# Channel attention: weighing in column quarters, and dividing after 32 by 32 transposes

## The chip, the cores and the metric

One core of a Trainium2 chip runs the whole program. The metric is the device time of one execution in microseconds, median of several. TensorE's clock is granted by the chip at one of two levels, 2.4 or 1.2 GHz; the profile shows the share granted (1.00 or 0.50).

## The reference, cut to what matters

Two layers of gated cross attention and feed-forward on x, 16 batch elements of 64 tokens by 256 features: gated attention, a mixture of experts, channel attention, a 4-bit MLP. The change is in the third, where the 64 tokens play the part of channels: 8 heads of 8 channels, and 256 features attend to 256 features.

```python
# q = layernorm(x), k = v = ctx_2048; per batch element 64 x 256
qh = q.reshape(B, 8, 8, 256)
kh = k.reshape(B, 8, 8, 256)
vh = v.reshape(B, 8, 8, 256)
qk = einsum('bhdq,bhdl->bhql', qh, kh) / sqrt(8)
ret = einsum('bhql,bhdl->bhdq', softmax(qk, axis=-1), vh)
x = x + tanh(g_xattn[1]) * gamma * ret.reshape(B, 64, 256)
```

## The kernel before, in words

Four stages follow one another; each is a block in which the five engines run their own instruction queues and wait for each other through semaphores. A tile of x holds two batch elements, i counts tiles, par is the half. The order of work in channel attention is written out by hand for each engine.

Per batch element, heads go in four pairs. For the next one it computes `row_scores` (L1504, matmuls at L1516: 32 rows of the array per head, since q and k are each split in a high and a low part and four products of 8 channels are laid side by side). VectorE reduces them to a maximum per query (`maxima`, L1676, L1684); the bank is reused, so the next pair's row scores wait for that. After four pairs `turn_maxima` (L1520, L1526) transposes the maxima and VectorE copies them to mT (`take_maxima`, L1689). For the present batch element TensorE computes `column_scores` (L1529): minus the maxima (L1539) plus the scores with keys on the partitions (L1544). ScalarE takes the exponent of each head's 512 columns (L1624). TensorE also replicates the rows of q and k for later pairs (`replicate`, L1492, L1499), which ScalarE copies (L1614).

`weigh` (L1549, L1559) multiplies values and exponents, contraction over 128 keys. Its stationary operand is a slice of vmask, 128 keys by 64 columns: the first 32 columns hold a head's 8 channels of values in the place of that head among four (zeros elsewhere), the other 32 hold ones in the same place. So PSUM rows 0 to 31 collect weighed values of four heads, rows 32 to 63 the sums of the exponents, once per channel; heads 4 to 7 do the same in rows 64 to 127. Both halves of the array's columns work on one pair of heads; four pairs accumulate. The matmuls are float32, and the profile shows two records for each: 8 for a pair, 32 for a batch element. The exponents have four buffers. vmask has a buffer per par, whose value columns GpSimd fills (`values`, L1650, L1659).

VectorE then inverts the sums (`invert`, L1691, two reciprocals of 128 columns over all 128 partitions, L1695), scales (`take_values`, L1697, two operations of 32 partitions, L1703) and adds to x (`add_values`, L1707, L1710). These stand between the maxima of the next batch element. At the end of the stage VectorE, ScalarE and GpSimd already begin the next stage's weights and its first statistics (`vector_stats_ahead`, L1106), which wait on `weighed`.

The order on TensorE for a batch element:

```python
for pair in range(C_HEADS // 2):
    row_scores(ni, npar, pair)
    column_scores(i, par, pair, first)
    if pair == 0: replicate(ni, npar, 1)
    if pair == 2: replicate(i + 1, par, 0)
    if pair >= 1: weigh(i, par, pair - 1, first)
turn_maxima(ni, npar)
weigh(i, par, C_HEADS // 2 - 1, first)
```

Of the kernel before, what the change touches and what calls it, by code (L numbers as in the profile page):

```python
# [15 lines left out]
ALU = mybir.AluOpType  # L16
# [9 lines left out]
P = 128  # L26
# [867 lines left out]
class Context:  # L894
# [3 lines left out]
    def __init__(self, nc, k, a, st):  # L898
        sb = lambda n, shape, dt: st.enter_context(nc.sbuf_tensor("context_" + n, shape, dt))
        self.nc, self.k, self.a = nc, k, a  # L900
        self.rows = sb("rows", [P, TILES, HID], F32)
        self.hi = sb("hi", [P, TILES, HID], F32R)
        self.lo = sb("lo", [P, TILES, HID], F32R)
        self.spread_in = sb("spread_in", [P, 16, P], F32)
        self.minus_in = sb("minus_in", [P, 2, P], F32)
        self.spread = sb("spread", [P, 16, P], F32R)
        self.minus = sb("minus", [P, 2, P], F32R)
        self.mx = sb("mx", [P, CH, P], F32)
        self.vmask = sb("vmask", [P, 2, CH, C_HEADS, 2 * C_ROWS], F32)
        self.rows_in, self.spread_arrived, self.minus_arrived, self.high, self.zeroed = [  # L910
            st.enter_context(nc.semaphore("context_" + n)) for n in ("rows_in", "spread_arrived", "minus_arrived", "high", "zeroed")]

# [20 lines left out]
    def gpsimd(self, pool):  # L933
        nc = self.nc
        nc.gpsimd.memset(self.vmask[:], 0.0).then_inc(self.zeroed, 1)
        nc.gpsimd.memset(self.mx[:], 0.0)
        pool.wait_ge(self.zeroed, 1)
        for par in range(2):
            for head in range(C_HEADS):
                col = C_ROWS + head % C_GROUP * C_DIM  # L940
                nc.gpsimd.memset(self.vmask[:, par, :, head, col:col + C_DIM], 1.0)


class Router:
# [100 lines left out]
class FourBitWeights:  # L1045
# [59 lines left out]

    def vector_stats_ahead(self, dve, x_done):  # L1106

        dve.wait_ge(x_done, 8)
        self.turn.vector_stats(dve, halves=(0,))

    def vector_ahead(self, dve):
# [330 lines left out]
def channel_attention(nc, k, a):  # L1442
# [8 lines left out]
    with ExitStack() as st:  # L1451
# [12 lines left out]

        qk_rows = sb("qk_rows", [P, 2, 2, 2, HID], F32R)
        mT = sb("mT", [P, HID], F32R)
        probs = sb("probs", [P, 4, 512], F32)
        inv = sb("inv", [P, HID], F32)
        part = sb("part", [P, HID], F32)
        s = {n: sem(n) for n in ("stats_done", "rstd_step", "row_normed", "c_turned", "c_copied", "h_high", "rest_high", "h_low", "gain_ready",  # L1470
                                 "rep_ready", "rep_copied", "a_ready", "a_reduced", "mt_ready", "mt_copied", "b_ready",
                                 "exp_done", "pv_done", "values_set", "inverted", "weighed", "out_taken")}
        A_BANK, B_BANK, REP_BANK, MT_BANK = 0, 2, 5, 6
        OUT_BANK = (4, 7)
        block = st.enter_context(nc.Block())
# [13 lines left out]
        def _(pe):  # L1489
# [56 lines left out]
                        if c == CH - 1:  # L1546
                            last.then_inc(s["b_ready"], 1)

            def weigh(i, par, pair, first=False):  # L1549

                pe.wait_ge(s["exp_done"], C_HEADS * (2 * i + par) + 2 * pair + 2)
                if pair == 0:
                    pe.wait_ge(s["values_set"], 2 * i + par + 1)
                    if not first:

                        pe.wait_ge(s["out_taken"], 2 * i + par - 1)
                for c in range(CH):
                    for e in range(2):
                        last = mm(ps[64 * e:64 * e + 64, OUT_BANK[par], 0:HID], vmask[:, par, c, pair + 4 * e, :],  # L1559
                                  probs[:, (2 * pair + e) % 4, c * HID:c * HID + HID],  # L1560
                                  start=(pair == 0 and c == 0), stop=(pair == C_HEADS // 2 - 1 and c == CH - 1))
                        if c == CH - 1:
                            last.then_inc(s["pv_done"], 1)

            def batch(i, par, first=False, scores_after=True, rows_after=True):
                ni, npar = (i, 1) if par == 0 else (i + 1, 0)
                for pair in range(C_HEADS // 2):
                    if scores_after:
                        row_scores(ni, npar, pair)
                    column_scores(i, par, pair, first)  # L1570
                    if pair == 0 and scores_after:

                        replicate(ni, npar, 1)
                    if pair == 2 and rows_after:
                        if first:

                            pe.wait_ge(s["h_low"], 2)

                        replicate(i + 1, par, 0)
                    if pair >= 1:  # L1580
                        weigh(i, par, pair - 1, first)
                if scores_after:
                    turn_maxima(ni, npar)
                weigh(i, par, C_HEADS // 2 - 1, first)

            for j in range(2 * CH):
                half, c = divmod(j, CH)
# [18 lines left out]
                batch(i, 1)  # L1606
            batch(LAST, 0, rows_after=False)
            batch(LAST, 1, scores_after=False, rows_after=False)

        @block.scalar  # L1610
        def _(act):
# [4 lines left out]
            def batch(i, par, first=False, scores_after=True, rows_after=True):  # L1616
                ni, npar = (i, 1) if par == 0 else (i + 1, 0)
                for head in range(C_HEADS):
                    n = C_HEADS * (2 * i + par) + head
                    act.wait_ge(s["b_ready"], n + 1)  # L1620
                    if not (first and head < 4):

                        act.wait_ge(s["pv_done"], n - 3)
                    nc.scalar.activation(probs[:, head % 4, :], ps[:, B_BANK + head % 2, :], ACT.Exp,  # L1624
                                         scale=float(C_DIM) ** -0.5).then_inc(s["exp_done"], 1)
# [23 lines left out]
        def _(pool):  # L1649
            def values(i, par, first=False):  # L1650
                if not first:

                    pool.wait_ge(s["pv_done"], C_HEADS * (2 * i + par - 1))

                flat = vmask[:, par].rearrange("p c h m -> p c (h m)")
                for head in range(C_HEADS):
                    col = head * 2 * C_ROWS + head % C_GROUP * C_DIM
                    src = cT[:].rearrange("p c (n b m) -> p c n b m", b=2, m=64)[:, :, i, par, head * C_DIM:head * C_DIM + C_DIM]
                    last = nc.gpsimd.tensor_copy(flat[:, :, col:col + C_DIM], src)  # L1659
                last.then_inc(s["values_set"], 1)  # L1660
# [14 lines left out]
        def _(dve):  # L1675
# [15 lines left out]
            def invert(i, par, part_of):  # L1691
                b = 2 * i + par
                dve.wait_ge(s["pv_done"], C_HEADS * (b + 1))
                cols = slice(part_of * P, part_of * P + P)
                nc.vector.reciprocal(inv[:, cols], ps[:, OUT_BANK[par], cols]).then_inc(s["inverted"], 1)  # L1695

            def take_values(i, par):  # L1697
                b = 2 * i + par
                dve.wait_ge(s["inverted"], CH * (b + 1))
                for half in range(2):  # L1700
                    rows, sums = [slice(at, at + C_ROWS) for at in (64 * half, 64 * half + C_ROWS)]
                    to = slice(64 * par + C_ROWS * half, 64 * par + C_ROWS * half + C_ROWS)
                    last = nc.vector.scalar_tensor_tensor(part[to, :], ps[rows, OUT_BANK[par], 0:HID], gain[rows, 0:1], inv[sums, :],  # L1703
                                                          ALU.mult, ALU.mult)
                last.then_inc(s["out_taken"], 1)

            def add_values(i, par):  # L1707
                mine = slice(64 * par, 64 * par + 64)
                dve.wait_ge(s["out_taken"], 2 * i + par + 1)
                nc.vector.tensor_tensor(x[mine, i, :], x[mine, i, :], part[mine, :], ALU.add).then_inc(s["weighed"], 1)  # L1710

            def finish(i, par):
                invert(i, par, 0)
                invert(i, par, 1)
                take_values(i, par)
                add_values(i, par)

            def batch(i, par, first=False, scores_after=True):
                ni, npar = (i, 1) if par == 0 else (i + 1, 0)
# [5 lines left out]
                if first:  # L1725
# [1 line left out]
                    dve.wait_ge(s["rest_high"], 1)  # L1727
                    nc.vector.tensor_tensor(h_lo[:, 1:TILES], h[:, 1:TILES], h_hi[:, 1:TILES].bitcast(F32), ALU.subtract
                                            ).then_inc(s["h_low"], 1)
                else:  # L1730
                    invert(*done, 0)
                maxima(ni, npar, 1)
                if not first:
                    invert(*done, 1)
                maxima(ni, npar, 2)
                if not first:
                    take_values(*done)
                maxima(ni, npar, 3)
                take_maxima(ni, npar)
                if not first:  # L1740
                    add_values(*done)

            row_stats(nc, dve, x, stats, mv, s["stats_done"], 0)
            nc.vector.tensor_scalar(gain[:], vec[:, S_GAMMA:S_GAMMA + 1], k.gain[:, 1:2], None, ALU.mult).then_inc(s["gain_ready"], 1)
# [14 lines left out]
            batch(LAST, 1, scores_after=False)  # L1759
            k.ffn.vector_ahead(dve)  # L1760
            finish(LAST, 1)


def build(nc, a, out, stages):
# [88 lines left out]
```

## Time and profile before

| | us |
|---|---|
| median of 3 runs | 1088.43 (1088.19 to 1090.18) |
| the profiled execution | 1089.46 |
| its span | 1087.70 |
| TensorE matmul busy | 981.8 (90%) |
| VectorE busy | 749.8 (69%) |
| ScalarE busy | 539.2 (50%) |
| GpSimd busy | 268.0 (25%) |
| mean granted clock | 0.947 |

PE is TensorE's matmuls, PEld its weight loads, DVE VectorE, ACT ScalarE, POOL GpSimd. Busy matmuls overlap, and their ends are modelled. A group "x8" in a timeline is eight records merged; "128*64" is rows by columns of the array that are in use. In square brackets stands how long the engine had been idle, and what ended it.

### The profile page before, as it was taken

What the parts mean: (1) busy time and instruction counts of PE and PEld (TensorE: products, weight loads), DVE (VectorE), ACT (ScalarE), POOL (GpSimd) and SP (SyncE); (2) the same over time, 40 slices, a digit from 0 to 9 for tenths busy, and PEclk for the clock granted to TensorE, in tenths of its full rate; (3) what the DMA queues carried; (4) which work ended last, traced back from release to release, by engine and by line L of the source; (5) the groups of instructions that cost most, each with busy time, mean ns of one, the idle gap of its engine ahead of it and who ended that gap; (6) DMA issues with size and microseconds to landing.
All of it is one profiled execution on the core that took longest, in us unless ns stands there. A gap on an engine that the chain in (4) does not pass through costs nothing. (4 is left out here: it accounts for less than half of the span.)

```text
span 1087.7 us, 19039 instructions
## 1 busy us (share of the span) xinstructions
PE 981.8 (90%) x6752; PEld 822.5 (76%) x6752; DVE 749.8 (69%) x1301; ACT 539.2 (50%) x1655; POOL 268.0 (25%) x416
## 2 busy tenths in 40 slices
PE   3689999999999999956899999995999999699998
PEld 3579999999999998855677777773666665577776
DVE  8858878777878787776544454445688888666653
ACT  5566666666666665622433333323455554233332
POOL 2133333333333333302422222202010111323130
PEclk8799999999999999976799999997899998799999
DMA  5001020101010100004111111001000000110001
GB/s 180 1 2 59 2 59 2 59 2 59 2 60 1 60 4 18 2 1 176 44 47 47 47 46 46 3 0 59 1 1 0 0 0 2 58 59 30 29 0 39
DMA packets 22823, 35.40 MB, mean 33 GB/s; under 512 B 2016, under 2 KB 19552, under 8 KB 21600
## 3 DMA queue, kind: packets, MB, share of 16 engines
q1 hardware_dynamic: 22464, 34.38, 9.6%
q8 instruction: 41, 0.67, 0.3%
q14 instruction: 30, 0.25, 0.1%
q10 hardware_dynamic: 288, 0.10, 0.0%
HBM read 33.42 MB, written 1.05 MB: 32 GB/s over the span
## 5 line engine op out<-in xcount | busy, mean ns | idle before, releaser
L251 PE MATMUL ps<-wt_hi,xq 128*128 128x256 f32 (+1 forms) x512 | 124.7, 278 | 13.0 <-issue 10.3
L251 PE MATMUL ps<-wt_lo,xq 128*128 128x256 f32 (+1 forms) x512 | 122.2, 281 | 0.0
L458 ACT ACTIVATE square<-ps 128x128 bf16<-128x128 f32 x384 | 100.6, 293 | 39.7 <-PE ps L251 39.6
L251 PEld LDWEIGHTS ps<-wt_hi,xq 128*128 128x128 f32 x512 | 98.4, 192 | 17.2 <-issue 15.3
L1624 ACT ACTIVATE ca_probs<-ps 128x512 f32<-128x512 f32 x128 | 69.5, 595 | 82.8 <-PE ps L1544 82.8
L251 PEld LDWEIGHTS ps<-wt_lo,xq 128*128 128x128 f32 x512 | 98.9, 193 | 0.0
L1684 DVE TENSOR_REDUCE context_mx<-ps 128x4 f32<-128x1024 f32 x64 | 76.9, 1201 | 26.4 <-PE ps L1516 26.4
L596 POOL TENSOR_TENSOR rstd<-rstd,half_neg 128x6 f32<-128x6 f32 x64 | 87.2, 1362 | 5.0
L1210 POOL TENSOR_TENSOR moe_w_lo<-moe_w_all,moe_w_hi 128x384 fp32r<-128x384 f32 x48 | 54.8, 1176 | 135.4 <-ACT moe_w_hi L1311 135.4
L458 ACT ACTIVATION_READ_ACCUMULATOR square<-ps 128x1 f32 x384 | 86.0, 225 | 0.0
L1375 DVE TENSOR_TENSOR moe_act_g<-moe_act_g,ps 128x512 f32<-128x512 f32 x48 | 33.0, 687 | 70.5 <-PE ps L1246 70.5
L669 DVE TENSOR_TENSOR qn<-ps,rstd 128x512 f32<-128x512 f32 x64 | 44.2, 690 | 49.4 <-POOL rstd L596 49.4
L1246 PE MATMUL ps<-moe_hT_hi,moe_w_hi 128*128 128x512 f32 x192 | 76.7, 399 | 0.6 <-POOL moe_w_lo L1210 0.6
L1327 ACT CAST moe_in_hi<-moe_inner 128x512 fp32r<-128x512 f32 x48 | 29.8, 621 | 94.6 <-DVE moe_inner L1378 82.7
L1246 PE MATMUL ps<-moe_hT_hi,moe_w_lo 128*128 128x512 f32 x192 | 75.8, 395 | 0.0
L1246 PE MATMUL ps<-moe_hT_lo,moe_w_hi 128*128 128x512 f32 x192 | 75.7, 394 | 0.0
L1559 PE MATMUL ps<-ca_probs,context_vmask 128*64 128x256 f32 x512 | 74.2, 415 | 0.0
L315 PE MATMUL ps<-wp_hi,catq 128*128 128x256 f32 x256 | 66.5, 298 | 7.2 <-DVE catq L93 7.2
L276 PE MATMUL ps<-kT,qT 128*128 128x64 f32 x512 | 64.2, 281 | 3.4 <-ACT kT L474 1.9
L276 PEld LDWEIGHTS ps<-kT,qT 128*128 128x128 f32 x512 | 62.3, 199 | 3.8 <-issue 2.1
L315 PE MATMUL ps<-wp_lo,catq 128*128 128x256 f32 x256 | 64.8, 292 | 0.0
L592 POOL TENSOR_TENSOR rstd<-sumsq,eps 128x6 f32<-128x6 f32 x64 | 15.1, 236 | 197.1 <-ACT square L458 197.1
(225 smaller groups left out, 2685.8 us busy)
## 6 DMA issues: line engine op xcount, KB each, us to landing
moe_w_all<-in_experts SPq DMA_DIRECT2D x8, 1152.0 KB, 5.4
wp_rows<-in_wproj SPq DMA_DIRECT2D x16, 256.0 KB, 2.9
ffn_codes<-in_codes SPq DMA_DIRECT2D x8, 384.0 KB, 3.2
ffn_w_scales<-in_code_scales SPq DMA_DIRECT2D x8, 384.0 KB, 3.9
w_rows<-in_wq SPq DMA_DIRECT2D x8, 256.0 KB, 3.7
w_rows<-in_wqx SPq DMA_DIRECT2D x8, 256.0 KB, 3.9
w_rows<-in_w_kv_x SPq DMA_DIRECT2D x16, 128.0 KB, 3.6
x_rows<-in_x SPq DMA_DIRECT2D x2, 512.0 KB, 5.1
```

Source lines behind the costliest of these rows:

```text
L251: last = mm(ps[:, first + bank, col:col + n], left[:, c, tokens], w[:, c, wcol:wcol + n], start=(j == 0), stop=(j == len(steps) - 1))
L276: last = mm(ps[:, S_BANK, b * SEQ:b * SEQ + SEQ], qT[:, r, batch].rearrange("p h s -> p (h s)"), kT[:, r, batch * SEQ:batch * SEQ + SEQ], ...
L315: last = mm(ps[:, CAT_BANK + j, q * HID:q * HID + HID], catq[:, f // HPG, f % HPG, t * P:t * P + P], w[:, f, :], start=(n == 0), stop=(n = ...
L458: last = nc.scalar.activation(square[:, j, :], ps[:, bank, (j % 4) * P:(j % 4) * P + P], ACT.Square, scale=float(HD) ** -0.5, accum_out=su ...
L596: nc.gpsimd.tensor_tensor(rstd[:, i % 2, :], rstd[:, i % 2, :], k.half_neg[:, 0:6], ALU.pow).then_inc(s["rstd_ready"], 1)
L669: nc.vector.tensor_tensor(qn[:, i % 2, 0:4, :], ps[:, bank, :].rearrange("p (h d) -> p h d", h=4), rstd[:, i % 2, 0:4].unsqueeze(2).broadc ...
L1210: last = nc.gpsimd.tensor_tensor(w_lo[:, b, cols], w_all[:, b, cols], w_hi[:, b, cols].bitcast(F32), ALU.subtract)
L1246: last = mm(ps[:, bank, :], w[:, b, col:col + P], h[:, c, tokens], start=(n == 0), stop=(n == len(steps) - 1))
L1375: nc.vector.tensor_tensor(act_g[:, half, :], act_g[:, half, :], ps[:, U_BANK, :], ALU.mult).then_inc(s["gated"], 1)
L1559: last = mm(ps[64 * e:64 * e + 64, OUT_BANK[par], 0:HID], vmask[:, par, c, pair + 4 * e, :], probs[:, (2 * pair + e) % 4, c * HID:c * HID ...
L1624: nc.scalar.activation(probs[:, head % 4, :], ps[:, B_BANK + head % 2, :], ACT.Exp, scale=float(C_DIM) ** -0.5).then_inc(s["exp_done"], 1)
L1684: nc.vector.tensor_reduce(dst, ps[:, A_BANK:A_BANK + 2, :].rearrange("p e (q l) -> p e q l", q=CH), AX.X, ALU.max).then_inc(s["a_reduced"], 1)
```

## The change

TensorE weighs four heads at a time, each in 32 of the array's 128 columns. The stationary operand is 128 keys by 32 columns: 16 columns hold the 8 channels of a head in one of two places, and one of the columns 16 and 17 holds ones, so a head's sum of exponents now takes one row of PSUM instead of eight. Quarter 2t + e holds heads 2 turn + t + 4 e for turn 0 and 1. There are two blocks of `weigh` per batch element instead of four: turn 0 at the end of its own batch, turn 1 in pair 1 of the next one. The exponents get a buffer for each of the 8 heads, and ScalarE waits for whole blocks.

Since sums and values now lie in different rows of one quarter, VectorE transposes the PSUM tile in blocks of 32 by 32 (`turn_values`), so that both lie in the columns of one partition; takes the reciprocals of 16 numbers per partition (`invert`); scales values by gain and reciprocal, writing them in the order of channels (`scale_values`, two operations of 64 partitions); and, once for two batch elements, transposes back (`turn_back`) and adds 128 rows to x. The count that `vector_stats_ahead` waits for follows, since `weighed` now rises once per tile. The diff, cut to its core:

```diff
-        self.vmask = sb("vmask", [P, 2, CH, C_HEADS, 2 * C_ROWS], F32)
+        self.vmask = sb("vmask", [P, 2, CH, C_HEADS, C_ROWS], F32)
...
-                col = C_ROWS + head % C_GROUP * C_DIM
-                nc.gpsimd.memset(self.vmask[:, par, :, head, col:col + C_DIM], 1.0)
+                col = 2 * C_DIM + head // 2 % 2
+                nc.gpsimd.memset(self.vmask[:, par, :, head, col:col + 1], 1.0)
...
-        probs = sb("probs", [P, 4, 512], F32)
-        inv = sb("inv", [P, HID], F32)
+        probs = sb("probs", [P, C_HEADS, 512], F32)
+        turned = sb("turned", [P, HID], F32)
+        inv = sb("inv", [P, HID // 32, 2], F32)
+        weighed = sb("weighed", [P, HID], F32)
...
+            def weigh(i, par, turn, first=False):
+
+                pe.wait_ge(s["exp_done"], C_HEADS * (2 * i + par) + 4 * turn + 4)
+                if turn == 0:
                     pe.wait_ge(s["values_set"], 2 * i + par + 1)
                     if not first:
 
                         pe.wait_ge(s["out_taken"], 2 * i + par - 1)
                 for c in range(CH):
+                    for quarter in range(4):
+                        t, e = divmod(quarter, 2)
+                        last = mm(ps[32 * quarter:32 * quarter + 32, OUT_BANK[par], 0:HID], vmask[:, par, c, 2 * turn + t + 4 * e, :],
+                                  probs[:, 4 * turn + quarter, c * HID:c * HID + HID],
+                                  start=(turn == 0 and c == 0), stop=(turn == 1 and c == CH - 1))
+                last.then_inc(s["pv_done"], 1)
...
+                done = (i - 1, 1) if par == 0 else (i, 0)
...
+                    if pair == 1 and not (first and par == 0):
+                        weigh(*done, 1)
...
-                    if pair >= 1:
-                        weigh(i, par, pair - 1, first)
+                weigh(i, par, 0, first)
                 if scores_after:
                     turn_maxima(ni, npar)
-                weigh(i, par, C_HEADS // 2 - 1, first)
...
+            weigh(LAST, 1, 1)
...
+                    if not first and head % 4 == 0:
+
+                        act.wait_ge(s["pv_done"], 2 * (2 * i + par) + head // 4 - 1)
+                    nc.scalar.activation(probs[:, head, :], ps[:, B_BANK + head % 2, :], ACT.Exp,
...
-                    pool.wait_ge(s["pv_done"], C_HEADS * (2 * i + par - 1))
+                    pool.wait_ge(s["pv_done"], 2 * (2 * i + par - 1))
...
+            def turn_values(i, par):
                 b = 2 * i + par
+                dve.wait_ge(s["pv_done"], 2 * (b + 1))
+                nc.vector.transpose(turned[:], ps[:, OUT_BANK[par], 0:HID]).then_inc(s["out_taken"], 1)
+
+            def invert(i, par):
+                dve.wait_ge(s["out_taken"], 2 * i + par + 1)
+                nc.vector.reciprocal(inv[:], turned[:].rearrange("p (b r) -> p b r", r=32)[:, :, 2 * C_DIM:2 * C_DIM + 2]
+                                     ).then_inc(s["inverted"], 1)
+
+            def scale_values(i, par):
+                dve.wait_ge(s["inverted"], 2 * i + par + 1)
+                to = slice(64 * par, 64 * par + 64)
+                for t in range(2):
+                    rows = slice(64 * t, 64 * t + 64)
+                    dst = weighed[to, :].rearrange("p (b r t d) -> p t b r d", r=2, t=2, d=C_DIM)[:, t]
+                    src = turned[rows, :].rearrange("p (b h r d) -> p h b r d", h=2, r=2, d=C_DIM)[:, 0]
+                    last = nc.vector.scalar_tensor_tensor(dst, src, gain[rows, 0:1],
+                                                          inv[rows].unsqueeze(3).broadcast_to([64, HID // 32, 2, C_DIM]),
                                                           ALU.mult, ALU.mult)
+                last.then_inc(s["scaled"], 1)
+
+            def turn_back(i):
+                dve.wait_ge(s["scaled"], 2 * i + 2)
+                nc.vector.transpose(part[:], weighed[:]).then_inc(s["turned_back"], 1)
+
+            def add_values(i):
+                dve.wait_ge(s["turned_back"], i + 1)
+                nc.vector.tensor_tensor(x[:, i, :], x[:, i, :], part[:], ALU.add).then_inc(s["weighed"], 1)
...
-                else:
-                    invert(*done, 0)
                 maxima(ni, npar, 1)
-                if not first:
-                    invert(*done, 1)
                 maxima(ni, npar, 2)
                 if not first:
-                    take_values(*done)
+                    turn_values(*done)
+                    invert(*done)
                 maxima(ni, npar, 3)
+                if not first:
+                    scale_values(*done)
                 take_maxima(ni, npar)
-                if not first:
-                    add_values(*done)
+                if not first and par == 0:
+                    turn_back(i - 1)
+                    add_values(i - 1)
```

## Rows read from the trace of the kernel before

**Rows 1.** The page: busy time, share of the span and instructions of each engine.
```profile
PE 981.8 (90%) x6752; PEld 822.5 (76%) x6752; DVE 749.8 (69%) x1301; ACT 539.2 (50%) x1655; POOL 268.0 (25%) x416
```

**Rows 2.** Timeline of a steady batch: start, length, engine, line, what; idle before.
```profile
834.22 0.51 PE L1516 MATMUL ps<-ca_qk_rows 32*128 32x256 f32 x4
...
834.77 1.23 DVE L1684 TENSOR_REDUCE context_mx<-ps 128x4 f32<-128x1024 f32 x1 [0.58 <-PE ps L1516]
...
835.30 1.09 ACT L1624 ACTIVATE ca_probs<-ps 128x512 f32<-128x512 f32 x2 [2.30 <-PE ps L1544]
...
836.05 0.50 PE L1516 MATMUL ps<-ca_qk_rows 32*128 32x256 f32 x4 [0.20 <-DVE context_mx L1684]
...
837.11 1.08 PE L1559 MATMUL ps<-ca_probs,context_vmask 128*64 128x256 f32 x8
...
838.13 0.50 PE L1516 MATMUL ps<-ca_qk_rows 32*128 32x256 f32 x4
...
844.06 0.51 PE L1516 MATMUL ps<-ca_qk_rows 32*128 32x256 f32 x4
```

**Rows 3.** Windows: length, busy time of PE, PEld, DVE, ACT, POOL, then granted clock.
```profile
760.00:765.00 5.00, 4.70 (x24) 3.65 (x26) 3.90 (x5) 1.67 (x3) 0.00 (x0) 0.50 0.00 0
765.00:770.00 5.00, 5.00 (x28) 3.12 (x24) 2.29 (x2) 2.11 (x4) 0.00 (x0) 0.50 0.00 0
772.00:775.00 3.00, 3.00 (x29) 1.84 (x28) 1.65 (x2) 1.09 (x2) 0.00 (x0) 1.00 0.00 0
910.00:912.00 2.00, 1.78 (x16) 0.92 (x14) 1.44 (x3) 0.95 (x2) 0.00 (x0) 1.00 0.00 0
912.00:914.00 2.00, 1.17 (x12) 0.54 (x8) 1.97 (x9) 0.79 (x2) 0.00 (x0) 1.00 0.00 0
914.00:916.00 2.00, 1.65 (x12) 1.15 (x14) 1.97 (x5) 1.18 (x3) 1.20 (x2) 0.83 0.00 0
916.00:918.00 2.00, 2.00 (x12) 0.99 (x10) 1.95 (x4) 0.26 (x2) 0.00 (x0) 0.50 0.04 8
918.00:920.00 2.00, 2.00 (x10) 0.86 (x12) 1.90 (x5) 1.02 (x2) 0.00 (x0) 0.50 0.00 0
```

**Rows 4.** Timeline at the granted clock 0.50, the stage's first scores and weighing.
```profile
760.30 0.69 PE L1526 MATMUL ps<-ident,context_mx 128*128 128x128 f32 x2 [1.33 <-DVE context_mx L1684]
...
760.92 0.80 PE L1516 MATMUL ps<-ca_qk_rows 32*128 32x256 f32 x4
...
765.39 1.98 PE L1559 MATMUL ps<-ca_probs,context_vmask 128*64 128x256 f32 x8
...
767.29 0.80 PE L1516 MATMUL ps<-ca_qk_rows 32*128 32x256 f32 x4
...
768.88 0.58 PE L1499 MATMUL ps<-ca_h_hi,context_spread 128*128 128x256 f32 x1
...
770.03 1.98 PE L1559 MATMUL ps<-ca_probs,context_vmask 128*64 128x256 f32 x8
```

**Rows 5.** Timeline of the stage's last batch.
```profile
916.69 0.79 PE L1539 MATMUL ps<-ca_mT,context_minus 32*128 32x512 f32 x2
...
917.84 1.98 PE L1559 MATMUL ps<-ca_probs,context_vmask 128*64 128x256 f32 x8
917.94 1.09 ACT L1624 ACTIVATE ca_probs<-ps 128x512 f32<-128x512 f32 x2 [1.74 <-PE ps L1544]
...
927.46 0.42 DVE L1710 TENSOR_TENSOR x_rows<-x_rows,ca_part 64x256 f32<-64x256 f32 x1
```

**Rows 6.** VectorE operations by tile: duration ns min/median/max, first and last start, forms.
```profile
L1695 DVE RECIPROCAL ca_inv<-ps x32: 894/944/958, 776.9 to 925.5; 128x128 f32<-128x128 f32 x32
L1703 DVE SCALAR_TENSOR_TENSOR ca_part<-ps,ca_gain,ca_inv x32: 471/478/483, 780.9 to 926.9; 32x256 f32<-32x256 f32 x32
...
L1689 DVE CAST ca_mT<-ps x16: 424/426/427, 761.0 to 911.5; 128x256 fp32r<-128x256 f32 x16
...
L1021 DVE RECIPROCAL route_col<-route_col x1: 203/203/203, 521.0 to 521.0; 128x8 f32<-128x8 f32 x1
```

More of the change, by code:

```diff
@@ L1106, in vector_stats_ahead @@
     def vector_stats_ahead(self, dve, x_done):
-        dve.wait_ge(x_done, 8)
+        dve.wait_ge(x_done, TILES // 2)
         self.turn.vector_stats(dve, halves=(0,))
@@ L1471, in channel_attention @@
                                  "rep_ready", "rep_copied", "a_ready", "a_reduced", "mt_ready", "mt_copied", "b_ready",
-                                 "exp_done", "pv_done", "values_set", "inverted", "weighed", "out_taken")}
+                                 "exp_done", "pv_done", "values_set", "inverted", "scaled", "turned_back", "weighed", "out_taken")}
         A_BANK, B_BANK, REP_BANK, MT_BANK = 0, 2, 5, 6
@@ L1547, in column_scores @@
                             last.then_inc(s["b_ready"], 1)
-            def weigh(i, par, pair, first=False):
-                pe.wait_ge(s["exp_done"], C_HEADS * (2 * i + par) + 2 * pair + 2)
-                if pair == 0:
+            def weigh(i, par, turn, first=False):
+                pe.wait_ge(s["exp_done"], C_HEADS * (2 * i + par) + 4 * turn + 4)
+                if turn == 0:
                     pe.wait_ge(s["values_set"], 2 * i + par + 1)
@@ L1557, in weigh @@
                 for c in range(CH):
[L1558 to L1563, printed above, removed]
+                    for quarter in range(4):
[4 more added lines that the diff above has]
+                last.then_inc(s["pv_done"], 1)
             def batch(i, par, first=False, scores_after=True, rows_after=True):
                 ni, npar = (i, 1) if par == 0 else (i + 1, 0)
+                done = (i - 1, 1) if par == 0 else (i, 0)
                 for pair in range(C_HEADS // 2):
@@ L1620, in batch @@
                     act.wait_ge(s["b_ready"], n + 1)
-                    if not (first and head < 4):
-                        act.wait_ge(s["pv_done"], n - 3)
-                    nc.scalar.activation(probs[:, head % 4, :], ps[:, B_BANK + head % 2, :], ACT.Exp,
+                    if not first and head % 4 == 0:
+                        act.wait_ge(s["pv_done"], 2 * (2 * i + par) + head // 4 - 1)
+                    nc.scalar.activation(probs[:, head, :], ps[:, B_BANK + head % 2, :], ACT.Exp,
                                          scale=float(C_DIM) ** -0.5).then_inc(s["exp_done"], 1)
@@ L1651, in values @@
                 if not first:
-                    pool.wait_ge(s["pv_done"], C_HEADS * (2 * i + par - 1))
+                    pool.wait_ge(s["pv_done"], 2 * (2 * i + par - 1))
                 flat = vmask[:, par].rearrange("p c h m -> p c (h m)")
                 for head in range(C_HEADS):
-                    col = head * 2 * C_ROWS + head % C_GROUP * C_DIM
+                    col = head * C_ROWS + head // 2 % 2 * C_DIM
                     src = cT[:].rearrange("p c (n b m) -> p c n b m", b=2, m=64)[:, :, i, par, head * C_DIM:head * C_DIM + C_DIM]
@@ L1689, in take_maxima @@
                 nc.vector.tensor_copy(mT[:], ps[:, MT_BANK, 0:HID]).then_inc(s["mt_copied"], 1)
-            def invert(i, par, part_of):
+            def turn_values(i, par):
                 b = 2 * i + par
[L1693 to L1703, printed above, removed]
-                                                          ALU.mult, ALU.mult)
-                last.then_inc(s["out_taken"], 1)
@@ L1707, in add_values @@
[L1707 to L1710, printed above, removed]
+                dve.wait_ge(s["pv_done"], 2 * (b + 1))
[4 more added lines that the diff above has]
+                                     ).then_inc(s["inverted"], 1)
@@ L1712, in finish @@
+            def turn_back(i):
[4 more added lines that the diff above has]
+                nc.vector.tensor_tensor(x[:, i, :], x[:, i, :], part[:], ALU.add).then_inc(s["weighed"], 1)
             def finish(i, par):
-                invert(i, par, 0)
-                invert(i, par, 1)
-                take_values(i, par)
@@ L1716, in finish @@
-                add_values(i, par)
+                turn_values(i, par)
+                invert(i, par)
+                scale_values(i, par)
             def batch(i, par, first=False, scores_after=True):
@@ L1761, in _ @@
             finish(LAST, 1)
+            turn_back(LAST)
+            add_values(LAST)
 def build(nc, a, out, stages):
```

## Prediction

> **What bounds the kernel now.** I read the page first: TensorE (PE) is busy 90% of the span, VectorE (DVE) 69% [rows 1]. The change touches one stage, channel attention, from about 745 to 928 us, so I went to the order of time in its steady state. One batch element (a "batch" below) takes from one `row_scores` of pair 0 to the next, 834.22 to 844.06, 9.85 us [rows 2]; there are 16. TensorE sets that pace: in a whole batch it waits only once, 0.20 us before 836.05, for the maxima [rows 2]. A block of `weigh` is one row of 8 matmul records, 837.11 to the next row at 838.13, 1.02 us [rows 2], four times per batch: 4.08 of 9.85 us. Two chains run close behind. The maxima: `row_scores` at 834.22, reduction 834.77 to 836.00, next `row_scores` at 836.05, so 1.83 us per pair at best. The exponents: 1.09 us per pair on ScalarE (ACT) from 835.30 [rows 2].
>
> Then the granted clock. The stage's first scores run at 1.2 GHz and the clock stays there from 760 to 770, though TensorE is busy 4.70 and 5.00 of 5 us; at 772 it is 2.4 GHz [rows 3]. At the end it falls: TensorE was busy 1.78 and 1.17 of 2 us in 910 to 914, in 914 to 916 the grant is mixed, and in 916 to 920 it is 1.2 GHz although TensorE is busy all the time [rows 3]. So in this stage being busy does not by itself bring the clock back, and I look at what TensorE ran in each stretch. From 760.92 to 765.39 it ran score matmuls on 32 of 128 rows and one `replicate`. From 765.39 to 771.93, just before the rise, it ran two weigh blocks of 1.90 and a `replicate` of 1.15: 4.95 of 6.54 us with all 128 rows in use [rows 4]. In the tail, score columns from 916.69 alternate with weigh blocks from 917.84, of 1.90 us again; 1.90 of each 3.05 us is weighing, and the clock stays down [rows 3, 5].
>
> **The change, part by part.** Weighing goes from four blocks of 8 records (64 columns of the array each) to two blocks of 16 records (32 columns each). The count of matmuls and weight loads per batch is the same; the gain exists if four quarters run beside each other as two halves did. *Block of 16:* not in the trace. From below, the block of 8 at the same clock, 1.02 or 1.90 us; from above twice that, 2.04 or 3.80 (quarters no better than halves). I take the lower end: halves and quarters are the same kind of splitting, and each quarter still has four records to run in a row as each half had. By the Trainium skill, page "TensorE: Matmul & The Clock Gate", Part 3, three column tiles gave 2.38 times one; by that efficiency, as an estimate, a block would be 2.4 us at 1.2 GHz and the sum below some 15 us higher.
>
> *Clock.* This decides. What the change removes from TensorE is exactly the work that uses the whole array, while the score matmuls on 32 rows stay. From the rows at 1.2 GHz: row and column scores of a pair 767.29 to 768.88, 1.59; `replicate` 768.88 to 770.03, 1.15; weigh block 765.39 to 767.29, 1.90; turning the maxima 760.30 to 760.92, 0.62 [rows 4]. A changed batch at that clock is 4 x 1.59 + 2 x 1.15 + 2 x 1.90 + 0.62 = 13.08 us. Of it 6.72 us (51%) is work on all 128 rows; the tail, which did not get its clock back, had 62%, and the stretch before the rise 76%. The scores begin at 1.2 GHz in both kernels, and nothing before 765.39 changes. So I forecast that the clock does not come back in this stage, or drops again soon, and that batches take 13.08 instead of 9.85 us.
>
> *VectorE, per batch.* Removed: two reciprocals of 128 columns, 0.94 each [rows 6], two scalings of 0.48 and an addition of 0.42, 3.3 us. Added: a transpose of 256 columns out of PSUM, a reciprocal of 16, two scalings of 128 columns, and every second batch a transpose and an addition of 128x256. The transposes are not in the trace: between 0.20 (the small reciprocal) and 1.9 (two big ones); I take 0.43, the copy of 128x256 from PSUM, the same shape and source. Reciprocal of 16: 0.20, that of 8 columns. Scaling: between 0.20 and 0.48; I take 0.35 [rows 6]. Sum 0.43 + 0.20 + 0.70 + (0.43 + 0.42)/2 = 1.76. With four maxima (4.9) and the copy (0.43) VectorE has 7.1 of 13.08 us to do: hidden at 1.2 GHz, even with each transpose at 1.9. If that cover went (full clock) it would cost up to 0.85 us every second batch, since `turn_back` and `add_values` stand ahead of the next maxima.
>
> *Waits.* `scale_values` is ahead of `take_maxima`, for which `column_scores` of the next batch waits; at 1.2 GHz the weigh block before `turn_maxima` covers it. ScalarE now waits for whole blocks of the batch before (8 buffers), which are long done. GpSimd's copies of the values wait for `pv_done` of the batch before last, and are next needed at the end of a batch: no cost. The memsets of a half-sized `vmask` lie in the expert stage on an engine with 75% idle: no cost. No DMA moves.
>
> **The sum**, against the profiled execution (1089.46 us, span 1087.70; 1.03 above the median of 1088.43).
> - First batch: both kernels start it at 760.92. Changed, it has one weigh block, at its end; the column scores of its third pair wait for the exponents of the second, whose columns end at 765.39: some 0.1 + 1.09 us, to 766.6 [rows 2, 4]. Then 1.0 (columns), 1.15, 1.59, 1.90 and 0.62, with 0.1 between: next batch at 772.95.
> - 13 batches of 13.08 and one of 11.93 (no `replicate` for a later pair): 954.9.
> - Last batch: no row scores; its pairs follow the exponent chain, 916.69 to 917.94 (1.25) and 1.09, 2.4 us each [rows 5]; with the weigh block in pair 1 the last exponent ends at about 965.5, two weigh blocks at 968.2, the VectorE chain (0.43, 0.20, 0.95, 0.43, 0.42 and waits) at 970.8.
> - Before, this was 927.88 [rows 5]. Difference +42.9; 1089.46 + 42.9 = 1132.4; less 1.0 to stand beside the median: **1131**. Own range, with 0.3 us a batch either way: 1124 to 1142.
>
> **Rivals.**
> *B, the clock holds 2.4 GHz (the other side).* For it: the stage before this and the steady state held it with some waits. Then a batch loses 2.04 us of weighing. Pairs 1 to 3, 836.05 to 844.06, go from 8.01 to 5.97, pair 0 stays 1.83: 7.80 [rows 2]. But the waits uncovered: pair 2 without its block is shorter than the maxima's 1.83 (+0.2), pair 0 waits for `take_maxima` and pair 1 for the exponents (+0.35), and every second batch for turn back and addition (+0.3 on average): 8.65. 14 batches from 772.95 end at 893.5, the last takes 13.5, so 907, 21 us less than now: 1067. It decides if TensorE, then with about 1.3 us of waits in 8.65, is enough to hold or regain the clock; against it, 1.17 of 2 us in 912 to 914 was followed by the fall [rows 3]. The Trainium skill, page "TensorE: Matmul & The Clock Gate", Part 1, says that activity releases the throttle and idle time sets it; read as plain busy time that gives this rival. Rows 3 speak against that reading: a TensorE that is busy throughout 916 to 920 stays at 1.2 GHz.
> *C, the clock goes to and fro.* Between B and the forecast in proportion: 1080 to 1120; even with before when a third of the stage is at 1.2 GHz.
> *D, the change doesn't do what it says:* quarters overlap no better than halves. Then a block is 3.80 and 31 blocks add 59 us to the forecast, 1190 (less at full clock, where the time would stay near 1090 with TensorE as busy as now).
>
> **Chances.** Forecast 0.60, B 0.22, C 0.14, D 0.04. The range 1064 to 1144 takes forecast, B and C with their bounds, and leaves out D and thin ends. Faster by over 0.2% (about what a measurement here can tell from no change): B and a third of C, 0.27; within 0.2%: 0.02; slower 0.71.
>
> **What would show it.** Right: granted clock 0.50 from 760 to 930 nearly throughout, `row_scores` of pair 0 every 13 us, TensorE without waits, the weigh block of 16 records 1.9 us long, VectorE idle before the maxima for TensorE, transposes of 0.4 us. Wrong: clock 1.00 over the stage with batches of 8 to 9 us and TensorE waiting for VectorE (B), the clock changing between windows (C), or a block of 16 near 3.8 us (D).

## The result, and the profile after

| | before | changed |
|---|---|---|
| median, us | 1088.31 | 1135.24 |
| range | 1087.04 to 1090.18 | 1131.59 to 1137.78 |
| profiled execution, span | 1089.46, 1087.70 | 1137.69, 1135.9 |
| mean granted clock | 0.947 | 0.868 |

The ratio is 1.0415, 95% interval 1.0392 to 1.0439: 4% slower. The page of the changed kernel, engines and granted clock in 40 slices (its first line answers to [rows 1]):

```profile
PE 1027.8 (90%) x6750; PEld 851.9 (75%) x6752; DVE 731.0 (64%) x1301; ACT 542.6 (48%) x1655; POOL 268.0 (24%) x416
...
PEclk8799999999999999776999999965555555799999
```

TensorE is busy for 46 us more, with the same number of matmuls and half as many blocks of weighing; VectorE for 19 us less. In slices 27 to 33, counted from 0 (767 to 965 us), the granted clock stands at 5 tenths. Windows over the stage, with the columns of [rows 3]:

```profile
760.00:765.00 5.00, 4.81 (x26) 3.75 (x26) 3.90 (x5) 1.67 (x3) 0.00 (x0) 0.50 0.01 3
765.00:770.00 5.00, 4.25 (x26) 3.36 (x26) 2.50 (x3) 2.76 (x5) 0.00 (x0) 0.50 0.00 0
780.00:800.00 20.00, 20.00 (x128) 12.63 (x124) 10.91 (x17) 8.26 (x15) 1.82 (x13) 0.50 0.00 1
...
904.00:908.00 4.00, 3.12 (x24) 1.96 (x22) 2.43 (x4) 1.56 (x3) 0.00 (x0) 0.90 0.00 0
908.00:920.00 12.00, 12.00 (x81) 7.51 (x78) 6.53 (x9) 4.37 (x9) 1.16 (x8) 0.51 0.00 0
```

The clock was down when the scores began, as before, and did not come back at 772. While there were scores to run it rose once, at 904.8, and fell again at 908.2; it rose a second time at 969.6, in the stage's last weighing, 0.2 us before TensorE was through with the stage. A batch in order of time, `row_scores` (now L1518) of pair 0 to that of the next:

```profile
852.08 0.80 PE L1518 MATMUL ps<-ca_qk_rows 32*128 32x256 f32 x4
...
852.19 0.42 DVE L1693 CAST ca_mT<-ps 128x256 fp32r<-128x256 f32 x1 [1.36 <-PE ps L1528]
...
852.75 0.79 PE L1541 MATMUL ps<-ca_mT,context_minus 32*128 32x512 f32 x2
...
855.05 0.80 PE L1518 MATMUL ps<-ca_qk_rows 32*128 32x256 f32 x4
...
856.63 1.94 PE L1562 MATMUL ps<-ca_probs,context_vmask 128*32 128x256 f32 x16
...
858.50 0.80 PE L1518 MATMUL ps<-ca_qk_rows 32*128 32x256 f32 x4
...
861.23 0.80 PE L1518 MATMUL ps<-ca_qk_rows 32*128 32x256 f32 x4
...
862.07 1.23 DVE L1688 TENSOR_REDUCE context_mx<-ps 128x4 f32<-128x1024 f32 x1 [0.87 <-PE ps L1518]
...
862.81 1.94 PE L1562 MATMUL ps<-ca_probs,context_vmask 128*32 128x256 f32 x16
...
864.68 0.69 PE L1528 MATMUL ps<-ident,context_mx 128*128 128x128 f32 x2
...
865.29 0.80 PE L1518 MATMUL ps<-ca_qk_rows 32*128 32x256 f32 x4
```

From 852.08 to 865.29 are 13.21 us, against 9.85 [rows 2] and a forecast of 13.08. Scores and `replicate` of a pair start at 852.08 and give way to the next at 855.05; a block of 16 records takes 1.87 us to the next row (856.63 to 858.50, 862.81 to 864.68), where 8 took 1.90 at this clock [rows 4]. The profile names no wait of TensorE's matmuls for another engine in the batch, and the maxima wait for it (0.87 us before 862.07). One short delay is there all the same: pair 0 takes 2.97 us (852.08 to 855.05), pair 2, with the same work, 2.73 (858.50 to 861.23). In pair 0 the column scores (852.75) begin 0.14 us after VectorE has copied the maxima (852.61); the changed order turns the maxima right before the next batch, with no block of weighing behind it to cover the copy. The profile names this wait where less stands before it: 0.16 us before 905.55, when the clock was up, and 0.52 us before 957.28, in the batch without row scores. VectorE's new work by tile (duration ns min/median/max), first what reads or writes `turned`, then `part`:

```profile
L1712 DVE SCALAR_TENSOR_TENSOR ca_weighed<-ca_turned,ca_gain,ca_inv x32: 332/349/987, 783.9 to 971.1; 64x128 f32<-64x128 f32 x32
L1698 DVE STREAM_TRANSPOSE ca_turned<-ps x16: 437/439/450, 781.2 to 969.9; 128x256 f32<-128x256 f32 x16
L1702 DVE RECIPROCAL ca_inv<-ca_turned x16: 252/252/254, 781.7 to 970.4; 128x16 f32<-128x16 f32 x16
```

```profile
L1719 DVE STREAM_TRANSPOSE ca_part<-ca_weighed x8: 445/445/446, 799.8 to 972.2; 128x256 f32<-128x256 f32 x8
L1723 DVE TENSOR_TENSOR x_rows<-x_rows,ca_part x8: 424/426/624, 800.4 to 972.6; 128x256 f32 x6, 128x256 f32<-128x256 f32 x2
```

And the end of the stage: the fourth row scores of the batch before the last, then score columns, weighing, the transposes and the addition to x:

```profile
952.36 0.80 PE L1518 MATMUL ps<-ca_qk_rows 32*128 32x256 f32 x4 [0.47 <-DVE context_mx L1688]
...
957.28 0.79 PE L1541 MATMUL ps<-ca_mT,context_minus 32*128 32x512 f32 x2 [0.52 <-DVE ca_mT L1693]
...
966.23 3.59 PE L1562 MATMUL ps<-ca_probs,context_vmask 128*32 128x256 f32 x32
...
969.90 0.45 DVE L1698 STREAM_TRANSPOSE ca_turned<-ps 128x256 f32<-128x256 f32 x1 [0.19 <-PE ps L1562]
...
972.17 0.45 DVE L1719 STREAM_TRANSPOSE ca_part<-ca_weighed 128x256 f32<-128x256 f32 x1
972.65 0.62 DVE L1723 TENSOR_TENSOR x_rows<-x_rows,ca_part 128x256 f32<-128x256 f32 x1
```

The last addition ends at about 973.3, before at 927.88 [rows 5]: 45.4 of the 48.2 us of span are lost in this stage. The other 2.8 us lie in the 4-bit MLP, which ran at 1.2 GHz for some 10 us at its start (before: 8) and once more for 3 us at 1000.

### The profile page after: what moved, and what is told of

The parts are those of the page before. It is cut to its first block and busy times, and to the rows that moved or that the text cites. A ratio compares the mean times of both kernels' runs of the same rounds, so it can differ in the third digit from the quotient of the medians.

```text
span 1135.9 us, 18925 instructions
## 1 busy us (share of the span) xinstructions
PE 1027.8 (90%) x6750; PEld 851.9 (75%) x6752; DVE 731.0 (64%) x1301; ACT 542.6 (48%) x1655; POOL 268.0 (24%) x416
## 5 line engine op out<-in xcount | busy, mean ns | idle before, releaser
L601 POOL TENSOR_TENSOR probs<-probs,total 128x512 f32<-128x512 f32 x32 | 33.5, 1047 | 122.7 <-DVE total L703 122.7
```

What stands on the lines that cost most here:

```text
L601: nc.gpsimd.tensor_tensor(probs[:, r], probs[:, r], total[:, r, :].unsqueeze(2).broadcast_to([P, 8, SEQ]), ALU.mult).then_inc(s["probs_rea ...
```

## The experiments

The question was whether the clock is the cause, or only goes along with work that is slow by itself (quarters, transposes, the new order). To move the clock alone, unread matmuls are put where TensorE mostly waits. They write to 256 columns of PSUM banks that nothing reads, so the result is computed as before:

```diff
+            def lead(n):
+                for _ in range(n):
+                    mm(ps[:, OUT_BANK[0], HID:2 * HID], spread[:, 0, :], c_hi[:, 0, :], start=True, stop=True)
+            def fill(i, par, n):
+                for _ in range(n):
+                    mm(ps[:, OUT_BANK[par], HID:2 * HID], spread[0:128, 0, :], h_hi[0:128, i, :], start=True, stop=True)
```

Each is 128 rows by 128 columns by 256; the runs with "32" in their name use `[0:32]` in `fill`.

**A first start, too weak: kick_hold, kick_hold32, kick, kick_before.** `fill(0, 0, 5)` after each `row_scores` of the four before the first batch; the "hold" runs also have `fill(i, par, 4)` after the first `replicate` of a batch and `fill(i, par, 2)` after the second.

> The changed kernel with extra matmuls whose result nobody reads, 128 rows by 128 columns by 256, into free columns of PSUM: 5 after each row_scores of the stage's first batch, where TensorE waits for the maxima anyway, and in every later batch 4 after the first replicate and 2 after the second. Clock theory (the array is used too little for the clock to come back): the granted clock is 1.00 from about 765 us on, a batch takes 8.6 to 9.3 us instead of 13.2, total 1065 to 1080. Rival (quarters, transposes and the new order cost the time themselves, the clock is a bystander): the time does not fall, and the added work makes it 1137 to 1150.

Measured: four executions, three at 1152.1 to 1156.9 with a mean granted clock of 0.862 to 0.867 and one at 1075.2 with 0.948. The start did not lift the clock in most executions. The one at 1075.2, which has no trace, was some 80 us below the others: the first sign that the changed kernel is quick at 2.4 GHz. The profiled one (1152.1) is at 1.2 GHz up to 964 and takes 14.5 us a batch: six unread matmuls of 128 rows in every batch cost 1.3 us there and did not bring the clock back. The median, 1154.4, missed the expectation.

> As kick_hold, in number, place and columns, but each extra matmul has 32 rows instead of 128 (a quarter of the array). Clock theory, with use of the array and not busy time as what counts: the clock stays at 0.50 as in the changed kernel, a batch takes 13.2 plus about 1.3 us, total 1148 to 1162. If it is TensorE's busy time that brings the clock back, this run is as fast as kick_hold.

Measured 1136.1 (1135.8 to 1136.8). The clock stayed low but for two rises of 3.4 us while there were scores to run, and the added matmuls cost less than expected, 1 us over the changed kernel instead of 13 or more: the trace shows the added matmuls running beside the row and column scores (the first of a batch starts at 866.44, the row scores at 866.45), and a batch takes 13.23 us.

> The changed kernel with the extra matmuls of the first batch alone (5 after each row_scores). Clock theory: the clock is 1.00 by about 760 us, drops within one to three batches, and does not come back; total within 15 us below the changed kernel, 1120 to 1137. If only the way in was missing (once at 2.4 GHz the stage holds it), 1060 to 1075.

Measured 1137.8, at the slow edge of what was expected. The clock was not up at the start (it rose for 3.4 us at 827 and at 905), so this tells little.

> The kernel before with the same extra matmuls of the first batch alone. Clock theory: the clock, which came back at 772, is there some 8 to 12 us earlier, and the kernel before holds it: 4 to 7 us faster, 1081 to 1085. Rival: no change, 1088.

Measured 1094.5, ratio 1.0052 (1.0035 to 1.0069): a miss, slower. Its trace has the clock back at 777 instead of 772, so the first batches ran longer at 1.2 GHz. The stage ends 2.2 us later than before (930.0 against 927.9); the rest of the loss lies in the next stage, where the clock falls once more, from 958 to 962. Why the added work did not bring the clock back sooner was not settled, and it speaks against the simple reading that more work on all rows is always enough.

**A strong start: lead_hold, lead_hold32, lead, lead_before.** While TensorE waits for the normed rows its clock is still at 2.4 GHz, and it falls in that gap (changed kernel: no matmul from 744 to 748, clock down at 748). The edit, on top of the above:

```diff
+            lead(40)
             pe.wait_ge(s["h_low"], 1)
             replicate(0, 0, 0, first=True)
...
                 row_scores(0, 0, pair, first=(pair == 0))
-                fill(0, 0, 5)
+                lead(8)
```

> The changed kernel with unread matmuls on the whole array: 40 right after the context is turned, while TensorE waits for the rows and its clock is still at 2.4 GHz, 8 after each row_scores before the first batch, and 4 + 2 in every later batch (as in kick_hold). Clock theory: the clock never falls before the last batch, a batch takes 8.6 to 9.3 us, total 1064 to 1078, in nearly every run. Rival (the new work itself is slow): at least 1130.

Measured: eleven executions, five at 1081.1 to 1089.8 (mean clock 0.933 to 0.947), six at 1148.3 to 1153.5 (0.868 to 0.873). The profiled one is of the second kind, its windows:

```profile
755.00:760.00 5.00, 4.21 (x35) 3.07 (x33) 4.45 (x5) 2.06 (x4) 0.00 (x0) 1.00 0.01 3
760.00:765.00 5.00, 3.90 (x30) 3.22 (x34) 3.14 (x3) 2.28 (x6) 0.00 (x0) 0.75 0.00 0
765.00:770.00 5.00, 5.00 (x32) 3.01 (x25) 1.92 (x3) 1.86 (x4) 0.00 (x0) 0.50 0.01 2
```

The clock was up to 760 and fell while TensorE was busy 3.90 of 5 us: in the first batch pair 1 has no weigh block and TensorE waits for VectorE, 1.63 us before 761.10. What was lost there did not come back in the stage, although the same 4 + 2 matmuls ran in every batch and TensorE was busy all the time (60 of 60 us from 800 to 860, batches of 14.5 us). The five shorter executions have no trace; that they kept the clock through this gap is an inference from their mean clock, and none reached the 1064 to 1078 that was expected.

> As lead_hold, but the 4 + 2 of every later batch have 32 rows. Clock theory, use of the array: the stage begins at 2.4 GHz, loses it within a few batches and stays at 0.50, 1125 to 1145. If busy time holds the clock, 1064 to 1078 as lead_hold.

Measured: five executions, three at 1114.5 to 1116.4 (clock 0.899 to 0.901), two at 1132.8 and 1133.2 (0.878 and 0.877). By the mean clock none kept it. The first three are faster than the expected 1125 to 1145; the profiled one (1133.2) lost the clock at 760 and, while it had scores to run, had it back twice for 3.4 us.

> The changed kernel with the 40 and 4 x 8 at the start alone. Clock theory: begins at 2.4 GHz, falls within one to three batches for want of work in the array and does not come back: 1120 to 1138. If the fall in the gap before the scores was all that was wrong: 1060 to 1075. Its batches at 2.4 GHz, while they last, measure rival B of the prediction, forecast at 8.65 us.

Measured 1132.9 (1131.5 to 1134.2); in its trace the clock, up at the start, falls at 762 and rises again only for 3.4 us at 929.6. Holding it, not only reaching it, is what the changed kernel lacks. The clock fell before a steady batch, so this run does not price one at 2.4 GHz.

> The kernel before with the 40 and 4 x 8 at the start alone. The first two batches run at 2.4 GHz and the kernel holds it as it does now: 4 to 9 us faster, 1079 to 1085. If the clock at the start is worth nothing to it: 1088.

Measured 1087.1, ratio 0.9985 (0.9974 to 0.9996): 2 us, less than expected. The clock fell for 6.8 us at 760 and came back at 767. The stage itself ends 4.6 us earlier than before (923.2 against 927.9), as expected; in the profiled execution 2.7 us of it are lost again in the next stage, whose clock falls once more at 951.

**The clock held throughout: held and held32.** On top of lead_hold, with 6 and 3 in place of 4 and 2:

```diff
                     if pair == 1 and not (first and par == 0):
                         weigh(*done, 1)
+                    if first and par == 0 and pair in (1, 3):
+                        fill(i, par, 12)
+                    if not scores_after:
+                        fill(i, par, 6)
```

> lead_hold lost the clock in the first batch, at pair 1 and 2, where TensorE waits 1.5 us for VectorE. This kernel fills that gap too: 12 unread matmuls on the whole array in pair 1 and in pair 3 of the first batch, 6 + 3 in every batch, 6 per pair in the last one. Clock theory: granted clock 1.00 from the start of the stage to its end in nearly every run, a batch of 8.6 to 9.2 us, total 1062 to 1078, faster than both kernels. Rival (new work is slow): 1130 or more. Rival B of the prediction put a batch at this clock at 8.65 us, with waits of TensorE for VectorE of 0.6 us every second batch.

Measured 1070.9 (1069.2 to 1071.7), ratio 0.9837 (0.9823 to 0.9851), five executions of one kind. Granted clock 1.00 up to 906, the end of the stage:

```profile
780.00:800.00 20.00, 19.57 (x215) 13.53 (x211) 15.38 (x22) 11.68 (x22) 2.94 (x21) 1.00 0.00 1
800.00:860.00 60.00, 58.37 (x605) 41.30 (x605) 47.65 (x70) 35.89 (x68) 7.40 (x52) 1.00 0.00 0
860.00:900.00 40.00, 37.46 (x393) 26.09 (x395) 31.22 (x54) 22.55 (x43) 5.79 (x34) 1.00 0.00 1
```

> The same number and places, but after the start (40 and 4 x 8 on the whole array) the unread matmuls have 32 rows. Clock theory, use of the array: the clock is lost in the first batches and the stage runs at 0.50 nearly throughout, 1125 to 1150. If busy time counts, 1062 to 1078 as held.

Measured 1116.0 (1115.3 to 1116.8), ratio 1.0250, faster than the expected 1125 to 1150. Its windows:

```profile
765.00:770.00 5.00, 5.00 (x39) 3.95 (x42) 1.51 (x2) 2.13 (x5) 0.00 (x0) 0.50 0.00 0
775.00:779.00 4.00, 4.00 (x40) 2.37 (x39) 1.38 (x2) 1.09 (x2) 0.49 (x4) 0.58 0.02 4
...
780.00:800.00 20.00, 19.57 (x215) 13.50 (x215) 16.34 (x26) 12.54 (x24) 2.30 (x16) 1.00 0.00 1
800.00:820.00 20.00, 19.57 (x205) 13.93 (x208) 15.53 (x22) 11.75 (x23) 2.30 (x16) 1.00 0.00 0
820.00:840.00 20.00, 19.72 (x175) 12.90 (x169) 13.56 (x20) 9.55 (x18) 2.29 (x16) 0.74 0.00 0
840.00:860.00 20.00, 20.00 (x135) 13.34 (x135) 9.04 (x14) 8.26 (x15) 1.77 (x13) 0.50 0.00 0
```

From 780 to 800 the two kernels show the same TensorE: 19.57 of 20 us busy, 215 matmuls, clock 1.00. The one with 128 rows keeps the clock to the end of the stage, the one with 32 loses it at 830 and does not get it back while it has scores to run, busy 20 of 20 us. Two things were not expected: it had lost the clock at 765 too and got it back at 778, right behind a block of weighing, with no unread matmul on more than 32 rows; and it then held it for some 50 us. Why it fell at 830 and not before the profile does not show. But number, places and columns are the same; only the rows in use differ, and 45 us hang on it. So busy time alone does not decide it.

What the clock's rises have in common can be read from the traces. In those of the kernel before, the changed kernel and the runs above and below, the clock rises 22 times between the start of the first batch and the end of the stage, each time while matmuls on all 128 rows run or within 0.6 us of their end: a block of weighing, the turning of the maxima that follows one (after: weighing 902.44, turning 904.30, rise 904.8), or twelve unread matmuls (held_before, 763). This fits the forecast's account. It does not say how much of such work is needed: most blocks of weighing are followed by no rise.

**The change at equal clock: held_before.** The kernel before with `lead(40)`, `lead(8)`, `fill(i, par, 12)` in pair 1 of the first batch and 6 in the last, none between.

> The kernel before with the start of held: 40 and 4 x 8 unread matmuls on the whole array, 12 in pair 1 of the first batch, 6 in the last; none in between, since the kernel before holds 2.4 GHz by itself. Gives the kernel before with the clock up from the start: 1078 to 1084. Against held (1070.9) it prices the change at equal clock: if halving the weigh blocks is worth what the steady batches say (9.85 against 8.93 us), this kernel is 8 to 15 us slower than held.

Measured 1083.2 (1083.1 to 1085.1), ratio 0.9965 (0.9951 to 0.9979). held is 12.4 us below it, though measured at another time; held_late below, measured beside it, is 11.8 us below, and the stage of the profiled execution ends 13.2 us earlier (907.4 against 920.6). So with the clock up in both (but for 3 us at 760 in held_before), the change gains 12 to 13 us, its unread matmuls in every batch included. The unread matmuls alone make the kernel before 4 us faster.

**What a batch costs at 2.4 GHz: held_late.** Two batches of held in order of time:

```profile
830.33 0.51 PE L1518 MATMUL ps<-ca_qk_rows 32*128 32x256 f32 x4
...
833.78 1.07 PE L1570 MATMUL ps<-ca_probs,context_vmask 128*32 128x256 f32 x16
...
837.60 1.07 PE L1570 MATMUL ps<-ca_probs,context_vmask 128*32 128x256 f32 x16
...
838.51 0.71 DVE L1728 SCALAR_TENSOR_TENSOR ca_weighed<-ca_turned,ca_gain,ca_inv 64x128 f32<-64x128 f32 x2
...
838.97 0.50 PE L1518 MATMUL ps<-ca_qk_rows 32*128 32x256 f32 x4
839.26 0.42 DVE L1709 CAST ca_mT<-ps 128x256 fp32r<-128x256 f32 x1
839.71 0.45 DVE L1735 STREAM_TRANSPOSE ca_part<-ca_weighed 128x256 f32<-128x256 f32 x1
...
839.82 0.49 PE L1541 MATMUL ps<-ca_mT,context_minus 32*128 32x512 f32 x2 [0.34 <-DVE ca_mT L1709]
...
840.65 1.22 DVE L1704 TENSOR_REDUCE context_mx<-ps 128x4 f32<-128x1024 f32 x1
...
841.92 0.51 PE L1518 MATMUL ps<-ca_qk_rows 32*128 32x256 f32 x4
...
848.18 0.51 PE L1518 MATMUL ps<-ca_qk_rows 32*128 32x256 f32 x4
```

830.33 to 838.97 is 8.64 us, 838.97 to 848.18 is 9.21, mean 8.93. A block of 16 starts at 833.78 and 837.60 and gives way after 1.01 us. In the second, the copy of the maxima (839.26) ends late behind `scale_values` (838.51), and the column scores wait 0.34 us for it; `turn_back` and the addition (839.71, 840.31) keep the first reduction to 840.65.

```diff
                 maxima(ni, npar, 0)
+                if par == 1 and not (isinstance(i, int) and i == 0):
+                    turn_back(i - 1)
+                    add_values(i - 1)
...
-                if not first and par == 0:
-                    turn_back(i - 1)
-                    add_values(i - 1)
```

> held with turn_back and add_values moved behind the first maxima of the next batch. In held every second batch takes 9.21 instead of 8.64 us, since the copy of the maxima and the next reduction come late on VectorE. If it is turn_back and add_values ahead of that reduction, batches even out near 8.7 and the total falls 2 to 5 us, 1066 to 1069; if it is scale_values ahead of take_maxima, nothing changes, 1070 to 1072. A risk: less waiting of TensorE cannot cost the clock, so no slower end is expected.

Measured 1071.5 (1071.4 to 1072.9), beside 1070.9: no gain.

```profile
838.68 0.71 DVE L1728 SCALAR_TENSOR_TENSOR ca_weighed<-ca_turned,ca_gain,ca_inv 64x128 f32<-64x128 f32 x2
...
839.15 0.50 PE L1518 MATMUL ps<-ca_qk_rows 32*128 32x256 f32 x4
839.42 0.42 DVE L1709 CAST ca_mT<-ps 128x256 fp32r<-128x256 f32 x1
839.76 1.22 DVE L1704 TENSOR_REDUCE context_mx<-ps 128x4 f32<-128x1024 f32 x1
...
839.98 0.49 PE L1541 MATMUL ps<-ca_mT,context_minus 32*128 32x512 f32 x2 [0.33 <-DVE ca_mT L1709]
...
841.01 0.45 DVE L1735 STREAM_TRANSPOSE ca_part<-ca_weighed 128x256 f32<-128x256 f32 x1
...
842.01 0.50 PE L1518 MATMUL ps<-ca_qk_rows 32*128 32x256 f32 x4
```

The reduction now starts at 839.76, 0.9 us earlier, but the next row scores (842.01) come 2.86 us after the last (839.15), 2.95 before. The column scores still wait 0.33 us for the copy behind `scale_values`; then come columns, `replicate` and six filling matmuls. The late reduction was covered by TensorE's own work. That moving `scale_values` behind `take_maxima` would gain was not tried.

## Why the prediction was right

*The clock decides.* Right, and it was the step of most weight. The forecast read three stretches of the trace before by what TensorE ran in them, and took it that score matmuls on 32 rows do not bring the clock back however busy TensorE is. held against held32 supports it with the rows alone changed: matmuls on 32 rows kept TensorE as busy and did not keep the clock. How much work on all rows brings it back is not shown; the shares that the forecast compared fit its three stretches and were not tested: kick_before added such work and got the clock back later, held32 regained it at 778 and lost it at 830. "Nearly throughout" was right: there are two short rises in the profiled execution, 3.4 us each, the second at the very end.

*A batch at 1.2 GHz:* 13.08 forecast, 13.21 measured. The difference is in pair 0, 2.97 instead of 2.74 us: the forecast took it that the wait for the maxima is covered by the block of weighing, but in the changed order nothing covers their copy. The block of 16 was taken at the lower end of 1.90 to 3.80 and measured 1.87; at 2.4 GHz 1.01, where 8 took 1.02 [rows 2]. Rival D is out, and four quarters lost nothing against two halves. The page "TensorE: Matmul & The Clock Gate" of the Trainium skill, Part 3, has three column tiles at 2.38 times one; these runs measured no single tile to compare, but the forecast's estimate of 2.4 us per block from it was too long.

*First batch:* the next was to start at 772.95, it started at 772.9, in part by luck: the wait in it that the profile names is not that for the exponents but 0.75 us of the third row scores for the maxima (at 766.09), and it happens to end as late: the exponents of the second pair end at 766.46, the columns of the third begin at 766.66. *VectorE:* transpose 0.44 (forecast 0.43), reciprocal 0.25 (0.20), scaling 0.35 (0.35), transpose back 0.45 and addition 0.43 (0.43, 0.42); hidden in the batches, but for the copy above. *End of the stage:* 970.8 forecast, 973.3 measured. The last batch begins 1.8 us late: batches of 0.13 more make 1.6; the batch before the last took 12.80 instead of 11.93, since without a `replicate` its fourth row scores waited for the maxima (0.47 us at 952.36), a wait that the forecast had at nothing; the rise at 904.8 gave back 0.65. The chain of VectorE at the end took 3.4 us from 969.90 instead of 2.6, with two scalings of 1.46 us in all and an addition of 0.62. *Total:* 1132.4 forecast for the profiled execution, 1137.7 measured; the stage gave 2.5 us of the gap and the next one, which was assumed unchanged, 2.8.

*Rival B* was priced at 8.65 us a batch and 1067 in all. held has 8.93 with nine unread matmuls in each batch and 1070.9. So its price was about right, and its condition, a clock that holds by itself, was what failed: lead began with it and lost it in the first batch, and where the changed kernel got it back in a steady batch (904 to 908, TensorE busy 3.12 of 4 us) it was gone within 4 us. The page "TensorE: Matmul & The Clock Gate" of the Trainium skill says in Part 1 that activity releases the throttle. Read as busy time, held32 does not agree: it stands at 0.50 with 20 of 20 us busy.

## What to carry to other kernels

When a change takes work out of TensorE, ask which part of the array the rest uses: a batch in which matmuls on 32 of 128 rows take half the time kept TensorE busy at 1.2 GHz and got the clock back only for 3.4 us, and 32 fewer full-width blocks turned a gain of 12 us at equal clock into a loss of 47. Where the work itself can't be packed on more rows, unread full-array matmuls in the waits can pay, if the clock is held from the start: with them the changed kernel runs at 1070.9, 1.6% below the kernel before. At 1.2 GHz they only cost time: 13 to 18 us in the longer executions of lead_hold. Check every gap, the one at the start of the stage first: the changed kernel did not recover a clock lost there but for short rises, the kernel before did after 24 us. Whether more full-array matmuls in each batch than the six of kick_hold, without the strong start, would bring it back was not tried.

## What was not expected of the hardware

With fillers of 32 rows the clock, lost at 765, came back at 778 and held for some 50 us before it fell at 830 (held32). One and the same kernel ran at 1081 to 1090 or at 1148 to 1153 us (lead_hold); in the longer execution that has a trace one gap in the first batch cost the clock. And five full matmuls in each of four waits made the kernel before 5.5 us slower (kick_before), with the clock back 5 us later than without them.
